# Bias sums over 64 rows in one product of ones, and the third tile's adapter transposed with the opening routing

## The chip, the cores and the metric

The kernel runs on one core of one Trainium2 chip. The metric is the device time of one execution in microseconds (us), here the median of three runs. The core has a matrix engine (TensorE, PE in the rows; its weight loads are PEld), a vector engine (VectorE, DVE), a scalar engine (ScalarE, ACT), GpSimd (POOL), and a queue engine (SyncE, SP) that issues most transfers. Each engine works through its own list in order; semaphores tie the lists together.

## The reference

Eight blocks (tiles) of 128 tokens, each token 512 wide. A first linear layer with a per-block low-rank adapter (rank 16), then a second layer whose output gets a contribution of two out of 16 experts per token, then the residual:

```python
lora_h = x @ A[slot]                                   # A, B chosen per block
y = x @ W.T + b + (lora_h @ B[slot]) * 2.0
base = y @ base_w.T + base_b
hidden = y @ A_ffn.T                                   # 64 wide
probs = softmax(y @ router_w.T)                        # 16 wide
topw, topi = top_k(probs, 2); topw = topw / (topw.sum() + 1e-6)
delta = sum_e combine[e] * (hidden @ B_ffn[e].T)
out = x + base + delta * 0.5
```

The first layer's bias `b` passes through the second layer, so each output column, and each column of `hidden` and of the router's logits, gets a constant: `sum_i b[i] * W2[i, n] + base_b[n]`, over 512 values of i.

## The kernel before, in words

**Folding.** W and the second layer's W2 (64 hidden, 16 router and 512 base columns: 592) are multiplied first, so that x meets one folded matrix P, 128 rows x 4 blocks k. All products run in a reduced-precision float format: each operand is split in a high part (a rounding copy, mostly on ScalarE) and a low part (value minus high, on VectorE or GpSimd), and each product is done as three: high x high, high x low, low x high. A pass over 592 columns is two matrix instructions of 296 columns, one for each half of a pair of PSUM banks (`halves`).

**Adapters.** C = B x W2 is made for all eight slots at once (`ps_c`, then `c_hi` and `c_lo`), and each tile's 16 rows are stacked by transfers into `c_stack`.

**Bias.** `bias_part_of(k)` on VectorE (L644) adds, for k = 0 to 3, the rows of W2 times the bias of their block into `bias_part` (128 rows x 592). What is left is a sum over 128 rows. It is split in `bp_hi` (ScalarE, L472) and `bp_lo` (VectorE, L679), and `bias()` on TensorE multiplies each with a matrix of ones, four matrix instructions of 296 columns. They stand in the last quarter of `x_other(0)`. ScalarE copies two rows of the sum (L549), VectorE makes the two constant rows of them (L693), which go into the first tile's adapter product and by a transfer (L315) into that of every other tile.

**Per tile t.** `x_first(t)` and `x_other(t)` are 12 matrix instructions each of 304 columns (4 blocks k, 3 products): the two halves of x P, the first with the adapter's 16 columns beside it. ScalarE and VectorE take these 16 columns out (`lora_hi`, L495; `lora_lo`, L701) in high and low parts beside each other in `routed`; TensorE turns them (`lora_transpose`, L960); ScalarE copies the result twice (`lora_t`, L502 and L503), and `lora_product(t)` (L970, L972) adds the adapter. VectorE takes out hidden and logits, makes the residual sum (`read_z`) and routes (`route`: maximum, two best, weights; exponentials in ScalarE's `exps`, L517). `routing_transpose(t)` (L990) turns hidden and weights of tile t. From t = 1 on it also turns the adapter part of tile t + 2, which then lies in the same tensor, so one transpose serves both; tiles 1 and 2 have a `lora_transpose` of their own. `routing_rows(t)` on ScalarE (L530, L531) copies the turned rows out; the weights go through memory (`spread_routing` on SP: out at L325, back in two copied forms at L338), VectorE multiplies them with hidden (`weigh`, L760) and the expert products of 512 columns follow in `iteration(t)`.

**What sets the order.** Everything is written out by hand, engine by engine: the order of the calls is the order of execution. The calls on TensorE around the change, in the main part:

```
x_first(0) x_other(0) lora_first_transpose x_first(1) lora_first_product x_other(1) lora_transpose(1)
x_first(2) routing_transpose(0) lora_product(1) x_other(2) lora_transpose(2) x_first(3) lora_product(2)
x_other(3) routing_transpose(1) x_first(4) ...
```

**GpSimd's list.** low part of x for tile 2, then a wait for `bp_lo` (`bpl_done`), low part of x for tile 3 (L380), adapter columns 2 (L390, L392), low part of the first expert quarter (L398), adapter 3, two more quarters, then for t = 4 to 7 adapter columns and low part of x. `x_first(4)` on TensorE waits for the low part of x of tile 4. VectorE makes one expert quarter itself (L657, behind `route(1)`).

Of the kernel before, what the change touches and what calls it, by code (L numbers as in the profile page):

```python
# [11 lines left out]
F32 = mybir.dt.float32  # L12
F32R = mybir.dt.float32r
# [5 lines left out]
P = 128  # L19
# [43 lines left out]
def adaln_ffn_kernel(nc, x_t, x_n, w_cat, tables, slots, b1, b2, experts, out):  # L63
    with ExitStack() as ctx:
        def sb(name, shape, dt=F32):
            return ctx.enter_context(nc.sbuf_tensor(name, shape, dt))
# [4 lines left out]
        def sem(name):  # L71
            return ctx.enter_context(nc.semaphore(name))
# [24 lines left out]
        c_hi = sb("c_hi", [P, W2N], F32R)  # L97
        c_lo = sb("c_lo", [P, W2N], F32R)
        bias_part = sb("bias_part", [P, W2N])
        bp_hi = sb("bp_hi", [P, W2N], F32R)  # L100
        bp_lo = sb("bp_lo", [P, W2N], F32R)
        bias_hi = sb("bias_hi", [FT, W2N], F32R)
        low_row = sb("low_row", [FT, 1])
        c_stack = sb("c_stack", [FT, NT, W2N], F32R)
# [104 lines left out]
        ch_done = sem("ch_done")  # L209
        cl_done = sem("cl_done")  # L210
        bias_step = sem("bias_step")
        bph_done = sem("bph_done")
        bpl_done = sem("bpl_done")
        pe_bias = sem("pe_bias")
# [204 lines left out]
        def _(act):  # L419
# [26 lines left out]
            def split_experts(q):  # L446
                js = slice(q * GC // 4, (q + 1) * GC // 4)
                act.wait_ge(in_exp[q], 16)
                nc.scalar.activation(e_hi[:, js, :], exp_raw[:, js, :], ACT.Copy).then_inc(eh_done, 1)
# [16 lines left out]
            x_hi_part(2)  # L466
            x_hi_part(3)
            split_experts(0)
            act.wait_ge(pe_c, 1)
            nc.scalar.activation(c_hi[:, :], w2_cols(ps_c), ACT.Copy).then_inc(ch_done, 1)  # L470
            act.wait_ge(bias_step, KC)
            nc.scalar.activation(bp_hi[:, :], bias_part[:, :], ACT.Copy).then_inc(bph_done, 1)  # L472
            def lora_first():
                z = z_lora[0]
                act.wait_ge(pe_first, 1)
# [10 lines left out]
            def lora_hi(t):  # L486
                z = z_lora[t % 2]
                act.wait_ge(pe_first, t + 1)

                if t in (3, 4):  # L490
                    act.wait_ge(pe_ht, t - 1)
                elif t >= 5:
                    act.wait_ge(pe_rt, t - 3)
                h_parts = routed[:, t % 2, T_H:P].rearrange("p (r b) -> p b r", b=2)
                nc.scalar.activation(h_parts[:, 0, :].bitcast(F32R), ps_z[t % 2][:, z:z + R], ACT.Copy,  # L495
                                     scale=LORA_SCALE).then_inc(hh_done, 1)
# [8 lines left out]
            def lora_t_alone(t):  # L505
                act.wait_ge(pe_ht, t + 1)
                lora_t(t, ps_ht)
# [49 lines left out]
            lora_hi(2)  # L557
            routing_rows(0)
            exps(1)
            lora_t_alone(2)  # L560
            act.wait_ge(in_xt[2], 16)
            x_hi_part(4)
            lora_hi(3)
# [27 lines left out]
        def _(dve):  # L591
# [46 lines left out]
            def bias_part_of(k):  # L638
                if k == 0:
                    dve.wait_ge(in_b, 32)  # L640
                    dve.wait_ge(first_set, 1)
                else:
                    dve.wait_ge(bias_step, k)
                nc.vector.scalar_tensor_tensor(out=bias_part[:, :], in0=w_raw[:, k, D:], scalar=b1_col[:, k:k + 1],  # L644
                                               in1=(b2_rows if k == 0 else bias_part)[:, :],
                                               op0=ALU.mult, op1=ALU.add).then_inc(bias_step, 1)

            def folded_lo(n):
                dve.wait_ge(ph_done, n + 1)
                m = FOLDS[n]  # L650
                nc.vector.tensor_tensor(p_lo[:, m, R:MVN], w2_cols(pairs[m]),
                                        p_hi[:, m, R:MVN].bitcast(F32), ALU.subtract).then_inc(pl_done, 1)

            def split_experts_lo(q):
# [6 lines left out]
            x_lo_early(1)  # L661
            bias_part_of(0)
            bias_part_of(1)
            folded_lo(0)
            folded_lo(1)
            dve.wait_ge(lbh_done, 1)
# [3 lines left out]
                                    ALU.subtract).then_inc(lbl_done, 1)  # L670
            folded_lo(2)
            folded_lo(3)
            bias_part_of(2)
            bias_part_of(3)
            dve.wait_ge(ch_done, 1)
            nc.vector.tensor_tensor(c_lo[:, :], w2_cols(ps_c), c_hi[:, :].bitcast(F32),
                                    ALU.subtract).then_inc(cl_done, 1)
            dve.wait_ge(bph_done, 1)
            nc.vector.tensor_tensor(bp_lo[:, :], bias_part[:, :], bp_hi[:, :].bitcast(F32),  # L679
                                    ALU.subtract).then_inc(bpl_done, 1)  # L680

            def lora_first_lo():
# [140 lines left out]
        def _(pe):  # L823
# [85 lines left out]
            def x_other(t):  # L909
                out_cols, cols = other_half[t % 2]  # L910

                x_side(t, out_cols, cols, bias_within=t == 0).then_inc(pe_x, 1)

            def x_side(t, out_cols, cols, bias_within=False):
                par = t % 2
                x_h, x_l = x_his[t % XB], x_los[t % XB]
                for k in range(KC):
                    if k == KC - 1 and bias_within:
                        bias()
                    if t == 0 and k == 0:  # L920
                        pe.wait_ge(pl_done, KC)
                    for n, (lhs, rhs) in enumerate(((x_h, p_hi), (x_h, p_lo), (x_l, p_hi))):
                        last = mm(ps_z[par][:, out_cols], lhs[:, k, :], rhs[:, k, cols],
                                  k == 0 and n == 0, k == KC - 1 and n == 2)
                return last

            def bias():
                pe.wait_ge(consts, 4)
                pe.wait_ge(bph_done, 1)
                pe.wait_ge(bpl_done, 1)  # L930
                halves(ps_b, BANK - W2H, W2H, ones[:, :], bp_hi[:, :], True, False)
                halves(ps_b, BANK - W2H, W2H, ones[:, :], bp_lo[:, :], False, True).then_inc(pe_bias, 1)

            def lora_first_transpose():
                pe.wait_ge(hh_done, 1)
# [16 lines left out]
            def lora_transpose(t):  # L952
                pe.wait_ge(hh_done, t + 1)
                pe.wait_ge(hl_done, t + 1)
                pe.wait_ge(ht_done, t)

                if t >= 2:
                    pe.wait_ge(ht_again_done, t - 1)
                    pe.wait_ge(rt_done, t - 1)
                nc.tensor.transpose(ps_ht, routed[:, t % 2, T_H:P], ident[:, :]).then_inc(pe_ht, 1)  # L960

            def lora_product(t):
# [13 lines left out]
            def routing_transpose(t):  # L976
                cols = SMALL
                pe.wait_ge(weights_done, t + 1)
                if 3 <= t + 2 < NT:
                    cols = P  # L980
                    pe.wait_ge(ht_set, 2)
                    pe.wait_ge(hh_done, t + 3)
                    pe.wait_ge(hl_done, t + 3)

                if t >= 1:
                    pe.wait_ge(rt_done, t)
                if t < 2:
                    pe.wait_ge(ht_done, t + 2)
                    pe.wait_ge(ht_again_done, t + 1)
                nc.tensor.transpose(ps_rt[0:cols, :], routed[:, t % 2, 0:cols], ident[:, :]).then_inc(pe_rt, 1)  # L990
# [44 lines left out]
            x_other(1)  # L1035
            lora_transpose(1)
            x_first(2)
            routing_transpose(0)
            lora_product(1)
            x_other(2)  # L1040
            lora_transpose(2)
            x_first(3)
            lora_product(2)
            x_other(3)
# [52 lines left out]
```

## Time and profile before

| | |
|---|---|
| three runs | 102.5, 101.35, 102.38 us; median 102.38 us |
| profiled execution | 101.29 us |
| its span, first to last instruction | 99.5 us |
| TensorE busy | 95.7 us, 96% of the span, 572 matrix instructions |
| VectorE, ScalarE, GpSimd busy | 66.0, 41.5, 21.4 us |
| chain that ended last | TensorE 93%, transfers 3% |

The profile is of one execution. The span leaves out 1.79 us of the execution's own time (101.29 - 99.5). Times in the rows below count from the span's start, in us. A matrix instruction's duration contains its way through the array; in an unbroken stream the distance from start to start is what it costs. A wait on TensorE holds the weight load that comes first.

### The profile page before, as it was taken

How to read it: one execution, taken by the hardware profiler on the slowest of the kernel's cores; microseconds unless marked ns; L12 is line 12 of the kernel's file. 1: busy time of each engine (PE TensorE's matmuls, PEld its weight loads, DVE VectorE, ACT ScalarE, POOL GpSimd, SP SyncE). 2: the span in 40 equal slices, each digit the busy share in tenths (PEclk: the TensorE clock that was granted, in tenths of full speed). 3: DMA queues.
4: the chain of work that ended last, by engine and by line, in shares of the span. 5: the costliest groups of instructions: out<-in, count | busy, mean ns of one | idle time of the engine just before them, and what ended most of it. 6: DMA issues, size and time to landing. Idle time of an engine off the chain costs nothing.

```text
span 99.5 us, 1812 instructions
## 1 busy us (share of the span) xinstructions
PE 95.7 (96%) x572; PEld 87.1 (87%) x572; DVE 66.0 (66%) x184; ACT 41.5 (42%) x101; POOL 21.4 (21%) x34
## 2 busy tenths in 40 slices
PE   6899999999999999999999999999999999999990
PEld 6799999999999999998898799887788787888980
DVE  5669996997475885995997577257949274572101
ACT  1713536878787545754442510551434031040000
POOL 4100004325999965107022000000000000000000
PEclk9999999999999999999999999999999999999999
DMA  2999669999357777892593472616237082020311
GB/s 47 337 362 389 188 132 338 303 403 362 78 93 195 209 227 158 235 209 56 142 243 114 128 204 102 213 37 194 107 95 234 25 232 84 0 105 0 112 53 53
DMA packets 8443, 16.92 MB, mean 170 GB/s; under 512 B 1571, under 2 KB 4131, under 8 KB 8434
## 3 DMA queue, kind: packets, MB, share of 16 engines
q1 hardware_dynamic: 7762, 16.41, 55.2%
q10 hardware_dynamic: 640, 0.40, 1.3%
q8 instruction: 5, 0.08, 0.4%
q14 instruction: 4, 0.03, 0.1%
q0 software_dynamic: 32, 0.00, 0.0%
HBM read 13.28 MB, written 2.16 MB: 155 GB/s over the span
## 4 chain that ended last, share of the span: by engine, by line
PE 93%; DMA 3%; DVE 0%; ACT 0%; issue 0%
PE pair L825 90%; DMA w_raw_all<-w_cat 3%; PE pair L970 1%; PE pair L972 1%; PE pair L990 1%; DVE xn L819 0%; ACT w_hi_all L425 0%; PE pair L960 0%; PE pair L949 0%; PE pair L947 0%; PE pair L939 0%
## 5 line engine op out<-in xcount | busy, mean ns | idle before, releaser
L825 PE MATMUL pair<-e_hi,w_hi_all 128*128 128x512 f32 (+1 forms) x72 | 27.1, 376 | 0.0
L825 PE MATMUL pair<-e_hi,w_lo_all 128*128 128x512 f32 (+1 forms) x72 | 26.7, 370 | 0.0
L825 PE MATMUL pair<-e_lo,w_hi_all 128*128 128x512 f32 (+1 forms) x72 | 26.7, 370 | 0.0
L538 ACT ACTIVATE w_hi_all<-exp_raw_all 128x512 fp32r<-128x512 f32 x16 | 9.7, 629 | 15.9 <-DVE exp_raw_all L760 15.8
L825 PEld LDWEIGHTS pair<-e_hi,w_lo_all 128*128 128x128 f32 x72 | 13.6, 188 | 2.5
L825 PEld LDWEIGHTS pair<-e_hi,w_hi_all 128*128 128x128 f32 x72 | 13.6, 188 | 2.5
L825 PEld LDWEIGHTS pair<-e_lo,w_hi_all 128*128 128x128 f32 x72 | 13.6, 189 | 2.0
L767 DVE TENSOR_TENSOR w_lo_all<-exp_raw_all,w_hi_all 128x512 fp32r<-128x512 f32 x16 | 10.4, 689 | 4.5 <-ACT w_hi_all L538 4.0
L760 DVE TENSOR_TENSOR exp_raw_all<-w_raw_all 128x512 f32<-128x512 f32 x16 | 11.0, 725 | 0.9 <-DMA w_raw_all<-spill 0.9
L774 DVE TENSOR_TENSOR xn<-pair,xn 128x512 f32<-128x512 f32 x7 | 4.8, 691 | 8.6 <-PE pair L825 8.6
L825 PE MATMUL pair<-p_hi,x_hi 128*128 128x304 f32 x32 | 10.0, 311 | 0.0
L825 PE MATMUL pair<-p_hi,w_hi_all 128*128 128x304 f32 x32 | 9.8, 308 | 0.0
L825 PE MATMUL pair<-p_lo,x_hi 128*128 128x304 f32 x32 | 9.7, 303 | 0.0
L825 PE MATMUL pair<-p_lo,w_hi_all 128*128 128x304 f32 x32 | 9.7, 302 | 0.0
L825 PE MATMUL pair<-p_hi,w_lo_all 128*128 128x304 f32 x32 | 9.7, 302 | 0.0
L825 PE MATMUL pair<-p_hi,x_lo 128*128 128x304 f32 x32 | 9.7, 302 | 0.0
L380 POOL TENSOR_TENSOR w_lo_all<-xt_raw,w_hi_all 128x512 fp32r<-128x512 f32 x4 | 5.2, 1297 | 14.5 <-ACT w_hi_all L443 11.4
L398 POOL TENSOR_TENSOR e_lo<-exp_raw_all,e_hi 128x1024 fp32r<-128x1024 f32 x3 | 7.2, 2400 | 0.0
L825 PE MATMUL pair<-w_hi_all 128*128 128x296 f32 x32 | 6.1, 301 | 0.4 <-ACT w_hi_all L425 0.4
L825 PEld LDWEIGHTS pair<-p_hi,w_hi_all 128*128 128x128 f32 x32 | 6.0, 188 | 0.3
L825 PEld LDWEIGHTS pair<-p_lo,w_hi_all 128*128 128x128 f32 x32 | 6.0, 189 | 0.2
L825 PE MATMUL pair<-w_lo_all,w_hi_all 128*128 128x296 f32 x32 | 6.1, 303 | 0.0
(107 smaller groups left out, 161.5 us busy)
## 6 DMA issues: line engine op xcount, KB each, us to landing
w_raw_all<-spill SPq DMA_DIRECT2D x16, 256.0 KB, 4.0
xt_raw<-x_t SPq DMA_DIRECT2D x4, 512.0 KB, 7.0
exp_raw_all<-experts SPq DMA_DIRECT2D x4, 512.0 KB, 8.4
xn<-x_n SPq DMA_DIRECT2D x4, 512.0 KB, 5.4
out<-xn SPq DMA_DIRECT2D x7, 256.0 KB, 2.8
w_raw_all<-w_cat SPq DMA_DIRECT2D x2, 552.0 KB, 6.5
c_stack<-c_hi SPq DMA_DIRECT2D x7, 74.0 KB, 3.8
c_stack<-c_lo SPq DMA_DIRECT2D x7, 74.0 KB, 4.2
```

The costliest lines, as they stand in the source:

```text
L380: pool.tensor_tensor(x_los[t % XB], xt_raw[:, t, :].rearrange("p (k n) -> p k n", k=KC), x_his[t % XB].bitcast(F32), ALU.subtract).then_in ...
L398: pool.tensor_tensor(e_lo[:, js, :], exp_raw[:, js, :], e_hi[:, js, :].bitcast(F32), ALU.subtract).then_inc(el_pool_done, 1)
L538: nc.scalar.activation(gt_hi[:, t % 2, js, :], g[:, js, :], ACT.Copy).then_inc(gh_done, 1)
L760: nc.vector.tensor_tensor(g[:, js, :], weight_rows[:, b, js, :], hidden[:, b, :].unsqueeze(1).to_broadcast([P, GH, P]), ALU.mult).then_inc ...
L767: nc.vector.tensor_tensor(gt_lo[:, t % 2, js, :], g[:, js, :], gt_hi[:, t % 2, js, :].bitcast(F32), ALU.subtract).then_inc(gl_done, 1)
L774: nc.vector.tensor_tensor(xn[:, t, :], ps_d[t % 2], xn[:, t, :], ALU.add).then_inc(out_done, 1)
L825: return nc.tensor.matmul(out_ap, lhs, rhs, start=first, stop=last)
L970: nc.tensor.matmul(ps_z[par][:, z_small[par]:BANK], ht[:, par, :], c_stack[0:HT, t, 0:border], start=False, stop=True, skip_group_check=True)
L972: nc.tensor.matmul(ps_z[par][:, BANK:BANK + W2N - border], ht[:, par, :], c_stack[0:HT, t, border:], start=False, stop=True, skip_group_ch ...
L990: nc.tensor.transpose(ps_rt[0:cols, :], routed[:, t % 2, 0:cols], ident[:, :]).then_inc(pe_rt, 1)
```

## The change

1. The bias sum is halved before it goes to TensorE. ScalarE copies the lower 64 rows of `bias_part` up to `bias_up`, VectorE adds the upper 64 rows, ScalarE takes the high part into rows 0 to 63 of `bp_split`, VectorE the low part into its rows 64 to 127. One product with ones then sums all 128 rows: two matrix instructions in place of four.
2. VectorE does `bias_part_of(2)` ahead of the folded low parts, no longer behind them. ScalarE's copy up stands ahead of `c_hi`.
3. `lora_transpose(2)` is gone. `routing_transpose(0)` now turns the adapter part of tile 2 too, in all 128 columns, and stands inside `x_other(2)` behind its first k; ScalarE's `lora_t(2)` reads it.

```diff
-        bp_hi = sb("bp_hi", [P, W2N], F32R)
-        bp_lo = sb("bp_lo", [P, W2N], F32R)
+        bias_up = sb("bias_up", [P // 2, W2N])
+        bp_split = sb("bp_split", [P, W2N], F32R)
...
@@ scalar
             split_experts(0)
+            act.wait_ge(bias_step, KC)
+            nc.scalar.activation(bias_up[:, :], bias_part[P // 2:, :], ACT.Copy).then_inc(bias_moved, 1)
             act.wait_ge(pe_c, 1)
             nc.scalar.activation(c_hi[:, :], w2_cols(ps_c), ACT.Copy).then_inc(ch_done, 1)
-            act.wait_ge(bias_step, KC)
-            nc.scalar.activation(bp_hi[:, :], bias_part[:, :], ACT.Copy).then_inc(bph_done, 1)
+            act.wait_ge(bias_added, 1)
+            nc.scalar.activation(bp_split[0:P // 2, :], bias_up[:, :], ACT.Copy).then_inc(bph_done, 1)
...
-                if t in (3, 4):
-                    act.wait_ge(pe_ht, t - 1)
-                elif t >= 5:
+                if t == 3:
+                    act.wait_ge(pe_ht, 2)
+                elif t >= 4:
                     act.wait_ge(pe_rt, t - 3)
...
             exps(1)
-            lora_t_alone(2)
+            lora_t(2, ps_rt[T_H:P, :])
...
@@ vector
             bias_part_of(1)
+            bias_part_of(2)
             folded_lo(0)
...
             folded_lo(3)
-            bias_part_of(2)
             bias_part_of(3)
+            dve.wait_ge(bias_moved, 1)
+            nc.vector.tensor_tensor(bias_up[:, :], bias_part[0:P // 2, :], bias_up[:, :],
+                                    ALU.add).then_inc(bias_added, 1)
             dve.wait_ge(ch_done, 1)
...
-            nc.vector.tensor_tensor(bp_lo[:, :], bias_part[:, :], bp_hi[:, :].bitcast(F32),
+            nc.vector.tensor_tensor(bp_split[P // 2:, :], bias_up[:, :], bp_split[0:P // 2, :].bitcast(F32),
                                     ALU.subtract).then_inc(bpl_done, 1)
...
@@ tensor
-                x_side(t, out_cols, cols, bias_within=t == 0).then_inc(pe_x, 1)
+                x_side(t, out_cols, cols, within=t in (0, 2)).then_inc(pe_x, 1)
...
+                    if k == 1 and t == 2 and within:
+                        routing_transpose(0)
...
-                halves(ps_b, BANK - W2H, W2H, ones[:, :], bp_hi[:, :], True, False)
-                halves(ps_b, BANK - W2H, W2H, ones[:, :], bp_lo[:, :], False, True).then_inc(pe_bias, 1)
+                halves(ps_b, BANK - W2H, W2H, ones[:, :], bp_split[:, :], True, True).then_inc(pe_bias, 1)
...
-                if 3 <= t + 2 < NT:
+                if t + 2 < NT:
                     cols = P
...
             x_first(2)
-            routing_transpose(0)
             lora_product(1)
             x_other(2)
-            lora_transpose(2)
             x_first(3)
```

VectorE between the early low parts of x and the first adapter part, before (L644 is a bias step, L651 a folded low part, L667 the adapters' low part, L676 `c_lo`, L679 `bp_lo`, L685 the first adapter part):

```order
L644 SCALAR_TENSOR_TENSOR bias_part<-w_raw_all,b_col,b_rows 128x592
L644 SCALAR_TENSOR_TENSOR bias_part<-w_raw_all,b_col,bias_part 128x592
L651 TENSOR_TENSOR p_lo<-pair,p_hi 128x592 x2
L667 TENSOR_TENSOR lb_lo<-lora_raw,lb_hi 128x8x4x16
L651 TENSOR_TENSOR p_lo<-pair,p_hi 128x592 x2
L644 SCALAR_TENSOR_TENSOR bias_part<-w_raw_all,b_col,bias_part 128x592 x2
L676 TENSOR_TENSOR c_lo<-pair,c_hi 128x592
L679 TENSOR_TENSOR bp_lo<-bias_part,bp_hi 128x592
L685 SCALAR_TENSOR_TENSOR h_first<-pair,h_first 128x16
```

and the same stretch of the changed kernel (whose lines have other numbers: L651 is the bias step, L658 the folded low part):

```order
L651 SCALAR_TENSOR_TENSOR bias_part<-w_raw_all,b_col,b_rows 128x592
L651 SCALAR_TENSOR_TENSOR bias_part<-w_raw_all,b_col,bias_part 128x592 x2
L658 TENSOR_TENSOR p_lo<-pair,p_hi 128x592 x2
L675 TENSOR_TENSOR lb_lo<-lora_raw,lb_hi 128x8x4x16
L658 TENSOR_TENSOR p_lo<-pair,p_hi 128x592 x2
L651 SCALAR_TENSOR_TENSOR bias_part<-w_raw_all,b_col,bias_part 128x592
L683 TENSOR_TENSOR bias_up<-bias_part,bias_up 64x592
L686 TENSOR_TENSOR c_lo<-pair,c_hi 128x592
L689 TENSOR_TENSOR bp_split<-bias_up,bp_split 64x592
L695 SCALAR_TENSOR_TENSOR h_first<-pair,h_first 128x16
```

One bias step has moved ahead of the folded low parts, and the addition stands between the last bias step and `c_lo`.

TensorE from the end of `x_first(2)` into `x_other(2)`, before (L990 is the routing transpose, L970 and L972 the adapter product of tile 1):

```order
L825 MATMUL pair<-p_hi,w_lo_all 128x304
L990 MATMUL pair<-ident,routed 80x128 [waits ht_again_done,ht_done,weights_done]
L970 MATMUL pair<-c_stack,ht 128x304 [waits stacked1,ht_set,stacked_bias,ht_again_done,ht_done]
L972 MATMUL pair<-c_stack,ht 128x288
L825 MATMUL pair<-p_hi,w_hi_all 128x304
L825 MATMUL pair<-p_lo,w_hi_all 128x304
```

and changed (L998 is the routing transpose):

```order
L835 MATMUL pair<-p_hi,w_lo_all 128x304
L978 MATMUL pair<-c_stack,ht 128x304 [waits stacked1,ht_set,stacked_bias,ht_again_done,ht_done]
L980 MATMUL pair<-c_stack,ht 128x288
L835 MATMUL pair<-p_hi,w_hi_all 128x304
L835 MATMUL pair<-p_lo,w_hi_all 128x304
L835 MATMUL pair<-p_hi,w_lo_all 128x304
L998 MATMUL pair<-ident,routed 128x128 [waits hl_done,ht_done,hh_done,ht_again_done,ht_set,weights_done]
```

The transpose has moved five instructions later and now waits for the adapter parts of tile 2 as well (`hh_done`, `hl_done`).

## Rows read from the trace of the kernel before

**Rows 1.** The page: granted TensorE clock in 40 slices of the span.

```profile
PEclk9999999999999999999999999999999999999999
```

**Rows 2.** Waits of TensorE: engine line waited for: us, times, longest.

```profile
PE pair L825 <- PEq L1090: 0.8, 1, 0.8
PE pair L825 <- ACT w_hi_all L425: 0.4, 1, 0.4
```

**Rows 3.** The chain that ended last, in order: start us, us, what.

```profile
32.62 0.11 PE pair L960
```

**Rows 4.** Timeline of TensorE: start us, us, engine line op out<-in xcount.

```profile
23.90 0.43 PE L825 MATMUL pair<-bp_hi,ones 128*128 128x296 f32 x2
...
24.44 0.30 PE L825 MATMUL pair<-p_hi,x_hi 128*128 128x304 f32 x1
...
30.39 0.27 PE L990 MATMUL pair<-ident,routed 128*80 128x128 f32 x1
```

**Rows 5.** Timeline of the weight loads: bias, `x_first(1)`, second k of `x_other(2)`, `x_first(4)`.

```profile
23.77 0.33 PEld L825 LDWEIGHTS pair<-bp_hi,ones 128*128 128x128 f32 x2
...
24.86 0.19 PEld L825 LDWEIGHTS pair<-p_hi,x_hi 128*128 128x128 f32 x1
...
31.06 0.19 PEld L825 LDWEIGHTS pair<-p_hi,w_hi_all 128*128 128x128 f32 x1
...
36.20 0.19 PEld L825 LDWEIGHTS pair<-p_hi,x_hi 128*128 128x128 f32 x1
```

**Rows 6.** Timeline of VectorE around the bias; in brackets idle before, and its releaser.

```profile
14.37 0.83 DVE L644 SCALAR_TENSOR_TENSOR bias_part<-w_raw_all,b_col,bias_part 128x592 f32<-128x592 f32 x1
16.12 1.60 DVE L651 TENSOR_TENSOR p_lo<-pair,p_hi 128x592 fp32r<-128x592 f32 x2 [0.91 <-ACT p_hi L453]
...
19.59 1.49 DVE L644 SCALAR_TENSOR_TENSOR bias_part<-w_raw_all,b_col,bias_part 128x592 f32<-128x592 f32 x1
...
22.72 0.78 DVE L679 TENSOR_TENSOR bp_lo<-bias_part,bp_hi 128x592 fp32r<-128x592 f32 x1
...
23.71 0.77 DVE L779 TENSOR_TENSOR c_stack<-pair,c_stack 16x592 fp32r<-16x592 f32 x1
```

**Rows 7.** Timeline of ScalarE in the same stretch.

```profile
19.68 1.06 ACT L449 ACTIVATE e_hi<-exp_raw_all 128x1024 fp32r<-128x1024 f32 x1
...
21.98 0.70 ACT L472 ACTIVATE bp_hi<-bias_part 128x592 fp32r<-128x592 f32 x1 [0.16 <-DVE bias_part L644]
```

**Rows 8.** Timeline of GpSimd, 19 to 36 us.

```profile
19.14 1.31 POOL L380 TENSOR_TENSOR w_lo_all<-xt_raw,w_hi_all 128x512 fp32r<-128x512 f32 x1 [1.77 <-ACT w_hi_all L443]
23.57 1.29 POOL L380 TENSOR_TENSOR w_lo_all<-xt_raw,w_hi_all 128x512 fp32r<-128x512 f32 x1 [3.12 <-DVE bp_lo L679]
...
25.12 0.32 POOL L392 TENSOR_TENSOR p_lo<-lora_raw,p_hi 128x64 fp32r<-128x64 f32 x1
...
33.36 1.22 POOL L392 TENSOR_TENSOR p_lo<-lora_raw,p_hi 128x64 fp32r<-128x64 f32 x1
34.55 1.28 POOL L380 TENSOR_TENSOR x_lo<-xt_raw,x_hi 128x512 fp32r<-128x512 f32 x1
```

**Rows 9.** Timeline of VectorE, 30 to 42 us.

```profile
30.80 0.18 DVE L701 SCALAR_TENSOR_TENSOR routed<-pair,routed 128x16 fp32r<-128x16 f32 x1 [1.34 <-ACT routed L495]
...
33.18 1.22 DVE L657 TENSOR_TENSOR e_lo<-exp_raw_all,e_hi 128x1024 fp32r<-128x1024 f32 x1
...
40.72 1.28 DVE L760 TENSOR_TENSOR exp_raw_all<-w_raw_all 128x512 f32<-128x512 f32 x2
```

**Rows 10.** Timeline of ScalarE, 30 to 32 us.

```profile
30.80 0.27 ACT L530 ACTIVATE w_raw_all<-pair 16x128 f32<-16x128 f32 x1
...
31.50 0.31 ACT L517 ACTIVATE probs<-routed,neg_max 128x16 f32<-128x16 f32 x1
```

**Rows 11.** Timeline of SP's queue, 31 to 36 us.

```profile
34.06 1.14 SPq L338 DMA_DIRECT2D w_raw_all<-spill x2
```

**Rows 12.** The transfers of L338, 16 of them, to landing.

```profile
DMA to landing us min/median/max: 3.4/4.0/5.5
```

More of the change, by code:

```diff
@@ L211, in adaln_ffn_kernel @@
         bias_step = sem("bias_step")
+        bias_moved = sem("bias_moved")
+        bias_added = sem("bias_added")
         bph_done = sem("bph_done")
@@ L910, in x_other, with x_side @@
                 out_cols, cols = other_half[t % 2]
-                x_side(t, out_cols, cols, bias_within=t == 0).then_inc(pe_x, 1)
-            def x_side(t, out_cols, cols, bias_within=False):
+                x_side(t, out_cols, cols, within=t in (0, 2)).then_inc(pe_x, 1)
+            def x_side(t, out_cols, cols, within=False):
                 par = t % 2
@@ L917, in x_side @@
                 for k in range(KC):
-                    if k == KC - 1 and bias_within:
+                    if k == KC - 1 and t == 0 and within:
                         bias()
+                    if k == 1 and t == 2 and within:
+                        routing_transpose(0)
                     if t == 0 and k == 0:
@@ L955, in lora_transpose @@
                 pe.wait_ge(ht_done, t)
-                if t >= 2:
-                    pe.wait_ge(ht_again_done, t - 1)
-                    pe.wait_ge(rt_done, t - 1)
                 nc.tensor.transpose(ps_ht, routed[:, t % 2, T_H:P], ident[:, :]).then_inc(pe_ht, 1)
```

## The prediction

> **What bounds the kernel now.** I read the page first: the granted TensorE clock stands at its full level, 2.4 GHz, in all 40 slices [rows 1], so no term below comes from the clock. The waits of TensorE come next: it waited twice in the whole execution, 0.8 us for the start and 0.4 us for the first split [rows 2]. From then on it runs without a gap to the last product. So TensorE's list of instructions is the time. A matrix instruction taken out gives back its distance from start to start; a wait put in front of one is paid in full; every other engine costs nothing until it makes TensorE wait. The rest of my reading is therefore the timeline, engine by engine, at the places that the change touches: how early is each thing that TensorE takes, and how much later does it come now.
>
> **What goes.** The four bias products start at 23.90 and the next product at 24.44 [rows 4]: 0.54 us for four, 0.135 each. Two go: -0.27. The lone transpose of tile 2 has 0.11 us on the chain [rows 3]: -0.11. The transpose that takes over its work has 128 columns of weights where it had 80, but streams the same 128 (30.39 in rows 4), so I add nothing for it; the bounds are nothing and the 0.11 of a whole transpose. Together -0.38, the gain if no wait appears.
>
> **The bias chain.** Before, it was: last bias step, high part on ScalarE, low part on VectorE. Now it is: last step, copy up, addition, high, low, all in a row, over four hand-overs between two engines.
> - The step that moves forward goes in front of the folded low parts at 16.12, where VectorE was idle for 0.91 us; a step takes 0.83 [rows 6]. It costs nothing; the cover is that gap, and a few hundredths more would only delay low parts.
> - The last step now starts where the last but one did, at 19.59. That instruction took 1.49 us there, 0.66 more than its like at 14.37 [rows 6], while GpSimd ran its own subtraction from 19.14 to 20.45 [rows 8]. The bounds are 0.83 and 1.49. I take 1.49, since the same operation on the same kind of tile meets the same GpSimd instruction at the same moment. It ends at 21.08. ScalarE is free since 20.74 [rows 7].
> - Half the rows don't make it cheaper: over 16 rows VectorE's subtraction took 0.77, over 128 rows 0.78 [rows 6]. A ScalarE pass over 592 columns took 0.70 [rows 7]. A hand-over is 0.04 (high part ends 21.98 + 0.70 = 22.68, low part starts 22.72). So: copy up 21.12 to 21.82, addition 21.86 to 22.64, high part 22.68 to 23.38, low part 23.42 to 24.20. Before, the low part ended at 23.50. The chain ends 0.70 later.
> - `c_hi` and `c_lo` fill the holes between (ScalarE from 21.8, VectorE from 22.6), and what stands behind them, the transfers of `c_stack`, are wanted only by `lora_product(1)`.
> - TensorE loads the bias weights at 23.77 [rows 5], now not before 24.24: a wait of 0.47. If the last step took 0.83, the load could go at 23.58 and there would be no wait. Bounds 0 and 0.47; I take 0.47. After the two products that went, TensorE is at +0.20.
>
> **What hangs on the chain.** `x_first(1)` loads at 24.86 [rows 5] and waits for the first tile's low adapter rows, 23.71 + 0.77 = 24.48 [rows 6], a slack of 0.38. Their place is behind `bp_lo`. If they shift by the whole 0.70 they are there at 25.18 + 0.04, and TensorE wants them at 24.86 + 0.20 = 25.06: 0.16 more. But before they stood 0.2 us off the end of `bp_lo`'s slot, so less than 0.70 reaches them. I take 0 and keep 0.16 for the range.
>
> **The routing transpose.** It now stands behind the first k of `x_other(2)`, whose second k loads at 31.06 [rows 5]. A transpose ahead of that is gone (-0.11) and TensorE is at +0.20: 31.15. It needs the low adapter part of tile 2, 30.80 + 0.18 = 30.98 [rows 9], which follows `x_first(2)` and so shifts by 0.20 as well: 31.18, with the hand-over 31.22. A wait of 0.07; bounds 0 and 0.15.
>
> **GpSimd's list.** It waits for `bp_lo` before its next subtraction, at 23.57 [rows 8], and is then packed up to the low part of x for tile 4, 34.55 to 35.83. Shifted by 0.70 that ends at 36.53. `x_first(4)` waits for it and loads at 36.20 [rows 5], now at 36.20 + 0.20 - 0.11 + 0.07 = 36.36. Whether that wait comes hangs on one instruction. GpSimd's short subtraction at 33.36 took 1.22 us where its like at 25.12 took 0.32 [rows 8]; VectorE's expert quarter ran from 33.18 to 34.40 [rows 9], started 0.18 earlier, and GpSimd's ended 0.18 behind it. Now both are later. GpSimd's comes at 34.06. VectorE's follows the routing of tile 1, which waits for ScalarE's exponentials, which now stand behind the copies of the later transpose: load 31.22, 0.13 to the product (23.77 to 23.90), 0.27 for it [rows 4], 0.04: 31.66 in place of 30.80; the exponentials 0.54 to 0.70 behind that, at 32.20 to 32.36 in place of 31.50 [rows 10]; so the expert quarter at 33.88 to 34.04. VectorE is still first, by 0.02 to 0.18. Then it holds GpSimd to 35.10 or later, the low part of x ends about 36.57, and TensorE waits 0.25. If GpSimd is first it saves its 0.90 and nobody waits. Bounds 0 and 0.37; I take 0.25.
>
> The Trainium skill, "SBUF — State Buffer", section "Who interferes with whom", has a rule for this: a VectorE instruction with two SBUF inputs and a GpSimd instruction that reads SBUF exclude each other, and the one that starts second is blocked for the whole of the first. By that rule, both long rows are blocked instructions (the trace agrees: 1.49 beside 0.83, 1.22 beside 0.32), and the sum below holds; if they were chance, the bias wait and the one at `x_first(4)` would both be absent and the sum would be -0.38 + 0.07.
>
> **The sum.** -0.27 - 0.11 + 0.47 + 0.07 + 0.25 = +0.41 us on the profiled execution's 101.29, so 101.7. With every wait at its lower bound it is -0.38, at its upper -0.38 + 0.63 + 0.15 + 0.37 = +0.77. Behind `x_first(4)` I cost nothing: GpSimd and ScalarE idle again before the low part of x for tile 5, and the 35 us of expert products have no wait to lengthen. The runs shown are 101.35, 102.38 and 102.5: the profiled execution lies with the fastest, 1.1 us under the median, and nothing in the profile says where a new median falls. I put the number between 101.7 and 102.38 + 0.41 = 102.8, at 102.2.
>
> **Rivals.**
> 1. Bias wait yes, `x_first(4)` no, because GpSimd gets in ahead of VectorE: +0.16. For it: the margin is a tenth of a us. On the two bases 101.45 to 102.55.
> 2. The waits stay away and the whole -0.38 is seen: 100.9 to 102.0. For it: the last bias step meets GpSimd only if GpSimd's subtraction isn't over; against it: nothing shifts that meeting, and the chain has two more passes and no slack left.
> 3. Slower by over 2%: the routing weights' way through memory. SP reads them back at 34.06 [rows 11], with 4.0 us median and 5.5 at most to landing [rows 12], and VectorE's first product with them stands at 40.72 without a gap [rows 9]. With the transpose's rows 0.86 later on ScalarE, the second of the two reads is issued about 35.5 and lands by 41.0 at the worst of the rows, against 41.1 wanted. From there each us late is up to a us of TensorE, which has nothing else to do before the expert products. To cost 2.05 us the landing must be at 43.2, 7.7 us after the issue; no row is that long.
> 4. That the change doesn't do what it says: the order shows two products and one transpose fewer, so I give it nothing of its own.
>
> **Chances and range.** Forecast 0.45, rival 1 0.33, rival 2 0.18, rival 3 0.02, the remaining 0.02 a gain over 2% that no term here makes. 2% (2.05 us) is about what a measurement of this kernel can tell from no change, and every case but the third is far inside it: same 0.96, faster 0.02, slower 0.02. The range runs from 101.0 (the profiled 101.29 less most of rival 2) to 103.1 (the slowest run, 102.5, with +0.6, the forecast with one more bound); the likeliest case's own is 101.6 to 102.9.
>
> **What would show it.** In the changed profile: the waits of TensorE list one for the low part of the bias at about 24.2, of some 0.45 us, and a small one at the moved transpose for VectorE's L711 or so; the bias step at 19.6 is 1.49 long; GpSimd's next subtraction starts at 24.2 to 24.3. A third wait of about 0.25 before the first product of `x_first(4)`, released by GpSimd, decides between the forecast and rival 1; there GpSimd's short subtraction near 34 is 1.2 or 0.3 long. The prediction is wrong if the addition and copy over 64 rows turn out shorter than over 128, if a step of the chain overlaps its neighbour, or if a wait appears in the expert stage.

## The result: half a microsecond slower

The changed kernel takes 102.54 us in the median of 22 runs, before 102.22 us in the median of 22: a ratio of 1.0049, 95% interval 1.0025 to 1.0073, or +0.5 us (the two medians alone differ by 0.32). Ratios, here and below, leave out executions more than 1.5% above their kernel's fastest. The change is within 2%, and clear of no change. The sum of the prediction was +0.41 on the profiled execution; the number that was written down, 102.2, lies under the median of 102.38 shown then, and so said "faster". The sign was lost after the sum, and three of its terms were off besides.

The profiled executions differ by 1.28 us (101.29 and 102.57), over twice the effect; their spans differ by 1.1 (99.5 and 100.6). Half of that is not the change: the first products of all, which nothing in it touches, went slower this time.

TensorE's first products, changed kernel (start us, us, what):

```profile
4.28 0.83 PE L835 MATMUL pair<-w_hi_all 128*128 128x296 f32 x2 [0.38 <-ACT w_hi_all L429]
4.90 0.69 PE L835 MATMUL pair<-w_lo_all,w_hi_all 128*128 128x296 f32 x2
5.40 0.69 PE L835 MATMUL pair<-w_hi_all,w_lo_all 128*128 128x296 f32 x2
```

and before:

```profile
4.25 0.51 PE L825 MATMUL pair<-w_hi_all 128*128 128x296 f32 x2 [0.35 <-ACT w_hi_all L425]
4.60 0.44 PE L825 MATMUL pair<-w_lo_all,w_hi_all 128*128 128x296 f32 x2
4.88 0.49 PE L825 MATMUL pair<-w_hi_all,w_lo_all 128*128 128x296 f32 x2
```

Two products that follow each other take 0.62 and 0.50 us from start to start (4.28 to 4.90 to 5.40) where before it was 0.35 and 0.28, and the same weight load, the first of `x_first(0)`, comes at 21.41 in place of 20.83. The views print a granted clock of 1.00, the upper level of 2.4 GHz, in this stretch of both traces, but there they have nothing to go by: the first clock entry in the trace, with 1.00, stands at 4.13 us before and at 6.06 us changed. In all eleven traces of this document that first entry lies between 4.12 and 6.64 us, and wherever the products behind 4.2 us run slow, they do so up to that entry: ahead of it one product of 296 columns takes 0.25 us from start to start, behind it 0.14. That is the pace of the lower level, 1.2 GHz, ahead of the entry (inferred from the pace; no entry gives the level there). What the engine did before is the same in both traces: thirteen products of constants from 0.78 to 3.89 us, then some 0.4 us of idling. So the start of an execution depends on when the clock rises, and the kernel before was profiled with almost the earliest rise of the eleven. The clock row of [rows 1] doesn't show this.

From here on I measure every trace from that load to the start of the last product: 96.56 - 20.83 = 75.73 us before, 97.70 - 21.41 = 76.29 changed, +0.56. That ruler leaves the start out, and its +0.56 lies within the interval of the ratio (+0.26 to +0.75 us).

**Where the 0.56 is.** The changed kernel's chain that ended last runs, between 20.26 and 24.88, no longer through TensorE but through the bias:

```profile
20.26 1.42 DVE bias_part L651
21.67 0.02 issue
21.69 0.71 ACT bias_up L474
22.40 0.02 issue
22.43 0.78 DVE bias_up L683
23.20 0.02 issue
23.23 0.71 ACT bp_split L478
23.94 0.02 issue
23.96 0.78 DVE bp_split L689
24.74 0.14 issue
24.88 0.93 PE pair L835 x5
```

The weight loads of the changed kernel, where TensorE's waits show (in brackets the idle time before):

```profile
24.85 0.30 PEld L835 LDWEIGHTS pair<-bp_split,ones 128*128 128x128 f32 x2 [0.46 <-issue]
...
25.85 0.19 PEld L835 LDWEIGHTS pair<-p_hi,x_hi 128*128 128x128 f32 x1 [0.22 <-issue]
...
31.38 0.19 PEld L980 LDWEIGHTS pair<-c_stack,ht 66*128 66x128 f32 x1
...
32.29 0.14 PEld L998 LDWEIGHTS pair<-ident,routed 128*128 128x128 f32 x1 [0.31 <-issue]
32.33 0.22 PEld L835 LDWEIGHTS pair<-p_hi,w_hi_all 128*128 128x128 f32 x1
...
37.34 0.19 PEld L835 LDWEIGHTS pair<-p_hi,x_hi 128*128 128x128 f32 x1
```

Against the load of `x_first(0)`, and against [rows 5], the bias weights come at 3.44 and not 2.94 (+0.50), `x_first(1)` at 4.44 and not 4.03 (+0.41, so 0.18 of it new, after the 0.27 of two products), the moved transpose 0.36 later than the row of loads in front of it would let it (31.38 and four steps of just under 0.14 give 31.93), and `x_first(4)` at 15.93 and not 15.37 (+0.56). So: -0.27 + 0.50 + 0.18 - 0.11 + 0.36 = +0.66, of which 0.1 comes back because the transpose runs beside the restart of the stream: the next load follows its own by 0.04 (32.29 to 32.33), where 0.14 is usual. That leaves the +0.56. `x_first(4)` did not wait: VectorE and GpSimd met otherwise than forecast.

VectorE and GpSimd, changed kernel, answering to [rows 6, 8, 9]:

```profile
20.17 1.49 DVE L651 SCALAR_TENSOR_TENSOR bias_part<-w_raw_all,b_col,bias_part 128x592 f32<-128x592 f32 x1
...
31.79 0.17 DVE L711 SCALAR_TENSOR_TENSOR routed<-pair,routed 128x16 fp32r<-128x16 f32 x1 [1.35 <-ACT routed L501]
...
34.80 1.22 DVE L664 TENSOR_TENSOR e_lo<-exp_raw_all,e_hi 128x1024 fp32r<-128x1024 f32 x1
```

```profile
19.72 1.31 POOL L384 TENSOR_TENSOR w_lo_all<-xt_raw,w_hi_all 128x512 fp32r<-128x512 f32 x1 [1.76 <-ACT w_hi_all L447]
...
34.60 0.32 POOL L396 TENSOR_TENSOR p_lo<-lora_raw,p_hi 128x64 fp32r<-128x64 f32 x1
34.88 2.29 POOL L384 TENSOR_TENSOR x_lo<-xt_raw,x_hi 128x512 fp32r<-128x512 f32 x1
```

GpSimd's short subtraction got in first (34.60, 0.32 long), but the next one, the low part of x itself, started 0.08 after VectorE's expert quarter and took 2.29 instead of 1.28. It ended at 37.17, 0.17 ahead of the load at 37.34. The rival "GpSimd gets in first and nobody waits" came true with the wrong reason: GpSimd saved 0.9 on the short subtraction and paid 1.0 one instruction later. And it got in first because VectorE was later than forecast: 34.80 is 34.22 on the time axis of before (0.58 of later start taken off), where 33.88 to 34.04 was worked out. The transposed rows, and with them the routing on VectorE, followed a transpose that waited 0.29 us longer than forecast.

### The profile page after: what moved, and what is told of

Read it like the earlier page. It is cut to its first block, busy times and chain, and to the rows that moved or that the text cites. A ratio compares the mean times of both kernels' runs of the same rounds, so it can differ in the third digit from the quotient of the medians.

```text
span 100.6 us, 1808 instructions
## 1 busy us (share of the span) xinstructions
PE 96.5 (96%) x569; PEld 87.4 (87%) x569; DVE 66.9 (67%) x185; ACT 41.9 (42%) x102; POOL 21.8 (22%) x34
## 4 chain that ended last, share of the span: by engine, by line
PE 85%; DVE 6%; DMA 3%; ACT 2%; issue 1%
PE pair L835 82%; DMA w_raw_all<-w_cat 3%; DVE p_lo L658 2%; DVE bias_part L651 1%; PE pair L998 1%; PE pair L978 1%; PE pair L980 1%; DVE bp_split L689 1%; DVE bias_up L683 1%; ACT bp_split L478 1%; ACT bias_up L474 1%; ACT p_hi L457 1%; DVE lb_lo L675 1%; DVE xn L829 0%; ACT w_hi_all L429 0%
## 5 line engine op out<-in xcount | busy, mean ns | idle before, releaser
L835 PE MATMUL pair<-w_hi_all,w_lo_all 128*128 128x296 f32 x32 | 6.3, 308 | 0.0
```

The source lines that it names most:

```text
L835: return nc.tensor.matmul(out_ap, lhs, rhs, start=first, stop=last)
```

## Experiments

Each was timed in five rounds beside the kernel before. "Ruler" is the stretch from the first load of `x_first(0)` to the last product, 75.73 us before, 76.29 changed.

**1. The bias part alone.** The transposes are put back:

```diff
-                    if k == 1 and t == 2 and within:
-                        routing_transpose(0)
...
             x_first(2)
+            routing_transpose(0)
             lora_product(1)
             x_other(2)
+            lora_transpose(2)
```

> Only the bias part of the change; the transposes stand as before. Theory A (the waits of the changed trace are the cost, each paid in full by TensorE): -0.27 for two products, +0.50 at the bias weights, +0.18 at x_first(1), nothing at the transposes: +0.4 us against before, ratio 1.004. Whether x_first(4) waits for GpSimd is open: it is 0 in the changed trace by 0.1 us. Rival B (the bias part is hidden and the moved transpose alone costs the time): -0.27, ratio 0.997, and no wait at the bias weights. Rival C (the difference is the first microseconds of an execution, which differ by 0.6 us between the two traces, not the change): ratio 1.000.

Measured: ratio 1.0099 (1.0055 to 1.0144), ruler 76.19, +0.46. Waits of 0.44 and 0.21 at the two loads, and at `x_first(4)` a small one:

```profile
36.54 0.14 PEld L999 LDWEIGHTS pair<-ident,routed 128*128 128x128 f32 x1
36.76 0.19 PEld L835 LDWEIGHTS pair<-p_hi,x_hi 128*128 128x128 f32 x1
```

The second load follows the first by 0.22, where 0.14 is usual: 0.08 of wait, for a low part of x that ends at 36.71 (the row 35.42, 1.29, below). Here it was GpSimd's first instruction, a copy, that VectorE's quarter held:

```profile
33.78 1.28 POOL L394 CAST p_hi<-lora_raw 128x64 fp32r<-128x64 f32 x1
35.13 0.32 POOL L396 TENSOR_TENSOR p_lo<-lora_raw,p_hi 128x64 fp32r<-128x64 f32 x1
35.42 1.29 POOL L384 TENSOR_TENSOR x_lo<-xt_raw,x_hi 128x512 fp32r<-128x512 f32 x1
```

Rival B (the bias part is hidden) falls, and so does rival C (only the start differs), since the ruler leaves the start out. The trace stands with theory A, but the runs are 0.5 us slower than the trace says.

**2. The transposes alone.** The bias is as before, four products and no fold of the rows.

> Only the transposes of the change; the bias as before. Theory A: -0.11 for the transpose that goes, and at the moved one a wait of 0.3 to 0.35 before its weights (of which some 0.08 is given back, since the transpose then runs beside the restart): +0.1 to +0.15 us against before, ratio 1.001. Rival B: the moved transpose costs all of the 0.5: ratio 1.005. If the wait is only what is late in data (adapter low part ready 30.98, load wanted 30.95), it is under 0.1 and the sum is about -0.05, ratio 0.9995.

Measured: ratio 1.0031 (0.9998 to 1.0065), ruler 75.87, +0.14. The load of the moved transpose:

```profile
31.80 0.14 PEld L989 LDWEIGHTS pair<-ident,routed 128*128 128x128 f32 x1 [0.31 <-issue]
```

A wait of 0.31 with no bias in the way, where lateness of the data alone would be under 0.1. So on the ruler the merge costs 0.14 where it was to give 0.11, and the two parts, +0.46 and +0.14, come to 0.60 against the +0.56 of both together. Rival B (0.5 for the transpose) falls on the ruler; the interval of the time can't tell 1.001 from 1.005.

**3. The same waits, another order.**

```diff
                 if t < 2:
                     pe.wait_ge(ht_done, t + 2)
                     pe.wait_ge(ht_again_done, t + 1)
+                if t == 0:
+                    pe.wait_ge(hl_done, 3)
```

(and the call ahead of it left out for t = 0).

> The changed kernel with the same waits at the moved transpose, but the one on tile 2's low adapter part called last. In the changed trace the low part is ready at 31.96 and the weights are loaded at 32.29, with two more wait instructions between. Theory A (after the wait that comes true last, TensorE still works through the waits behind it, about 0.1 us each): the gap before the weights shrinks from 0.31 to 0.1 to 0.2, and the time by 0.1 to 0.2 us against the changed kernel. Rival (the semaphore itself comes late): the gap stays 0.3.

Measured: ratio 1.0046 (1.0011 to 1.0081), ruler 76.57. The loads:

```profile
31.09 0.19 PEld L980 LDWEIGHTS pair<-c_stack,ht 66*128 66x128 f32 x1
...
31.79 0.14 PEld L1001 LDWEIGHTS pair<-ident,routed 128*128 128x128 f32 x1
...
37.00 0.19 PEld L835 LDWEIGHTS pair<-p_hi,x_hi 128*128 128x128 f32 x1 [0.17 <-POOL x_lo L384]
```

From L980 to the transpose it is 0.70 us, in the changed kernel 0.91 (31.38 to 32.29), without a wait 0.55. So the wait is 0.15 and not 0.36: 0.21 us went by the order of the calls alone. In this trace the low part is ready at 31.68 and the load follows 0.11 later, where it was 0.33 in the changed kernel (31.96 to 32.29). The time doesn't show it, and the ruler went up by 0.28, for two other reasons. In this execution the last bias step was held for longer,

```profile
19.56 1.82 DVE L651 SCALAR_TENSOR_TENSOR bias_part<-w_raw_all,b_col,bias_part 128x592 f32<-128x592 f32 x1
```

since GpSimd's subtraction began 0.12 ahead of it and not 0.45 (it waits for a copy on ScalarE, which here waited 0.22 us for the transfer of x). The bias load waited 0.78, 0.32 more. And `x_first(4)` waited 0.17 for GpSimd, the wait that the prediction had put there: with the transpose earlier, VectorE's quarter comes just ahead of GpSimd's short subtraction, the meeting that was forecast.

```profile
34.30 1.21 DVE L664 TENSOR_TENSOR e_lo<-exp_raw_all,e_hi 128x1024 fp32r<-128x1024 f32 x1
```

```profile
34.33 1.36 POOL L396 TENSOR_TENSOR p_lo<-lora_raw,p_hi 128x64 fp32r<-128x64 f32 x1
```

Together +0.32 + 0.17 - 0.21 = +0.28, the whole difference. So most of what the order of the waits gives back at the transpose was lost again at `x_first(4)`.

**4. Without the two extra passes.**

```diff
-            act.wait_ge(bias_step, KC)
-            nc.scalar.activation(bias_up[:, :], bias_part[P // 2:, :], ACT.Copy).then_inc(bias_moved, 1)
...
-            nc.scalar.activation(bp_split[0:P // 2, :], bias_up[:, :], ACT.Copy).then_inc(bph_done, 1)
+            nc.scalar.activation(bp_split[0:P // 2, :], bias_part[0:P // 2, :], ACT.Copy).then_inc(bph_done, 1)
```

> The changed kernel without ScalarE's copy up and VectorE's addition; the rows 64 to 127 of the bias partial sums are left out of the result. Two bias products, as changed. Theory A (the two extra passes are what is late; 0.70 + 0.78 + two hand-overs on a slack of 0.27, less the bias step that no longer stands in the way): no wait at the bias weights and none at x_first(1); against before -0.27 - 0.11 + what the moved transpose waits (0.3): -0.1 us, ratio 0.999, 0.6 us under the changed kernel. Rival (the late thing is the last bias step, held by GpSimd's subtraction): the step is at 1.49 us still, the chain ends as before, since before it had the same step; so this rival needs a wait to remain, of 0.2 or more.

Measured: ratio 1.000 (0.9972 to 1.0027), ruler 75.61, -0.12, no wait at the bias load nor at `x_first(1)`. Theory A gave -0.1. With the passes the same kernel is 0.68 slower on the ruler: that is what the copy and the addition cost as long as GpSimd holds the last bias step, which is 1.48 long here too. So the rival (the held step alone) falls.

**5. GpSimd kept away from the bias step.**

```diff
             lora_a_parts(1)
-            x_lo_part(2)
             pool.wait_ge(bpl_done, 1)
+            x_lo_part(2)
             x_lo_part(3)
...
             split_experts_lo(1)
-            split_experts_lo(3)
             for t in range(4, NT):
                 lora_a_parts(t)
                 x_lo_part(t)
+                if t == 4:
+                    split_experts_lo(3)
```

> The changed kernel, with GpSimd's low part of x for tile 2 held until the low part of the bias is done (so that it can't meet the last bias step), and GpSimd's expert quarter 3 moved behind the low part of x for tile 4. Theory A (the two engines exclude each other): the last bias step is 0.83 long, not 1.49; the bias weights wait under 0.1 in place of 0.5, x_first(1) not at all in place of 0.2; the moved transpose still 0.36; x_first(4) between 0 and 0.4, since GpSimd's low part of x then runs beside VectorE's expert quarter. From the first product of x_first(0) to the end: 75.73 us before, 76.29 changed, here 75.7 to 76.1. Rival (1.49 is the length of a step that late in the program, for another reason): the step stays 1.49 and the waits stay.

Measured: ratio 0.9991 (0.9959 to 1.0024), ruler 76.05. VectorE's last bias step, and three weight loads (bias, `x_first(1)`, `x_first(5)`):

```profile
20.06 0.83 DVE L651 SCALAR_TENSOR_TENSOR bias_part<-w_raw_all,b_col,bias_part 128x592 f32<-128x592 f32 x1
```

```profile
24.23 0.33 PEld L835 LDWEIGHTS pair<-bp_split,ones 128*128 128x128 f32 x2
...
25.17 0.19 PEld L835 LDWEIGHTS pair<-p_hi,x_hi 128*128 128x128 f32 x1
...
40.73 0.19 PEld L835 LDWEIGHTS pair<-p_hi,x_hi 128*128 128x128 f32 x1 [0.34 <-POOL x_lo L384]
```

0.83 in place of 1.49, so the rival falls, and the bias load has no wait: all four passes fit if the step isn't held. `x_first(1)` still waits 0.11, where I had expected nothing: its load follows the one before by 0.24 (24.93 to 25.17), without a wait 0.13. So 0.50 and 0.07 came back, and 0.34 of that turned into a new wait at `x_first(5)`, behind the quarter that I had moved; I had looked for it at `x_first(4)`.

**6. The bias part alone, with GpSimd's list reordered** (the second half of the diff of experiment 5).

> The bias part of the change alone, as in the run before, with GpSimd's expert quarter 3 moved behind the low part of x for tile 4. That run was 1.0099 of before, 0.5 us more than its trace shows (+0.46). Theory A (x_first(4) waits for GpSimd in most executions, and the traced one was a lucky one): with the low part secured the ratio falls to about 1.004. Rival (the surplus is in the first microseconds, where the clock or the first transfers differ from execution to execution): the ratio is 1.004 to 1.010 all the same and runs over the fastest show a longer start, not a wait.

Measured: ratio 1.0023 (0.999 to 1.0057), ruler 76.10, no wait at `x_first(4)`. The ratio fell, as theory A has it, but the two intervals just touch, the trace gained 0.09 only, and both this kernel and the one before had runs over 1.5 us above their fastest. The experiment decides nothing: what makes the runs of experiment 1 slower than their trace stays open.

**7. The transposes alone, with two waits in place of six.**

```diff
-                    pe.wait_ge(ht_set, 2)
-                    pe.wait_ge(hh_done, t + 3)
+                    if t >= 1:
+                        pe.wait_ge(ht_set, 2)
+                        pe.wait_ge(hh_done, t + 3)
                     pe.wait_ge(hl_done, t + 3)
...
-                if t < 2:
+                if t == 1:
                     pe.wait_ge(ht_done, t + 2)
```

> The bias as before, the transposes changed, and the moved transpose waiting only for the routing weights and the low adapter part (the other four conditions follow from waits that stand before it). Theory A (each wait instruction behind the one that comes true last costs TensorE 0.1 us): the gap before its weights shrinks from 0.31 to about 0.1, and from the first product of x_first(0) to the end it takes 75.6 to 75.7 us, against 75.87 with all waits and 75.73 before. In the time 0.999 of before, which five rounds can hardly tell. Rival (the data are late): the gap stays 0.3.

Measured: ratio 1.0025 (0.9981 to 1.0069), ruler 75.66, -0.07. Loads:

```profile
30.39 0.19 PEld L971 LDWEIGHTS pair<-c_stack,ht 66*128 66x128 f32 x1
...
31.09 0.14 PEld L990 LDWEIGHTS pair<-ident,routed 128*128 128x128 f32 x1
```

0.70 from one to the other, a wait of 0.15: as with the low part called last. The low part is ready at 30.97, 0.12 ahead of the load, so the rival (late data) falls. The merged transpose is worth its 0.07 only with a short list of waits; the ratio, with 1 inside its interval, can't tell such a difference.

**8. The whole change, with experiments 5 and 7.**

> The whole change with GpSimd's list reordered as in the first of these four and the moved transpose with two waits. Theory A: bias wait under 0.1, none at x_first(1), about 0.1 at the transpose, 0 to 0.4 at x_first(4): from x_first(0) to the end 75.5 to 75.9 us, ratio to before 0.998 to 1.002. If TensorE's waits just move on to x_first(4) in full, 76.2 and 1.005.

Measured: ratio 0.9983 (0.9954 to 1.0012), ruler 75.85, with the 0.34 at `x_first(5)` again, 0.15 at the transpose and 0.12 at `x_first(1)`, where none was expected.

**9. The same, with the fourth expert quarter on VectorE,** in the gap behind the routing of tile 2:

```diff
             read_z(2)
             route(2)
+            split_experts_lo(3)
             lora_lo(4)
```

(GpSimd's call of it is gone, and TensorE waits for VectorE's count in its place.)

> The kernel of e9_all with expert quarter 3 moved from GpSimd to VectorE, behind the routing of tile 2, where VectorE was idle for 1.3 us. In e9 the one wait left over 0.15 was 0.34 at x_first(5), for the low part of x for tile 5, which stood behind that quarter on GpSimd. Theory A (each wait of TensorE is paid in full and nothing else counts): that wait goes, and from the first product of x_first(0) to the end it takes 75.5 us, against 75.85 in e9, 75.73 before and 76.29 changed; ratio to before about 0.998, which five rounds can show only just. Rival (the wait moves on, to low adapter part 4 behind the new VectorE pass, or to the expert stage): 75.8 or more.

Measured: 101.54 us against 101.89, ratio 0.9961 (0.9927 to 0.9994), ruler 75.57. This one is faster than the kernel before. The ruler, -0.16, shows less than half of the 0.4 us. The changed kernel wasn't timed beside it; on the ruler it is 0.72 behind. The rival (75.8 or more) falls. Its weight loads and the new pass:

```profile
24.40 0.33 PEld L834 LDWEIGHTS pair<-bp_split,ones 128*128 128x128 f32 x2
...
25.09 0.13 PEld L950 LDWEIGHTS pair<-ident,h_first 128*98 128x98 f32 x1
25.40 0.19 PEld L834 LDWEIGHTS pair<-p_hi,x_hi 128*128 128x128 f32 x1 [0.18 <-issue]
```

```profile
37.56 1.22 DVE L662 TENSOR_TENSOR e_lo<-exp_raw_all,e_hi 128x1024 fp32r<-128x1024 f32 x1
38.86 0.17 DVE L709 SCALAR_TENSOR_TENSOR routed<-pair,routed 128x16 fp32r<-128x16 f32 x1
```

The quarter fits between the routing and the next adapter part. What is left is 0.18 at `x_first(1)` and 0.15 at the transpose. The 0.18 is ScalarE's: the bias step is done at 21.05, but the copy up stands behind an expert quarter.

```profile
20.16 1.06 ACT L451 ACTIVATE e_hi<-exp_raw_all 128x1024 fp32r<-128x1024 f32 x1
21.25 0.70 ACT L472 ACTIVATE bias_up<-bias_part 64x592 f32<-64x592 f32 x1
```

Added up as above (what the list saves, each wait of TensorE in full, 0.1 back at the transpose), the waits give the ruler of each of the nine experiments to within 0.04 us. The ratios are further off it, from -0.4 us (experiment 5) to +0.5 (experiment 1), with intervals of 0.3 to 0.45 us to either side; the start, which the ruler leaves out, can be a part of that, and how large a part isn't shown.

## Why the prediction was wrong, and where it was right

- **The number.** The failed step is the last of "The sum". It had +0.41 on the profiled execution, and then put the time half way between two bases, 101.29 and 102.38, which took 0.55 off and turned the sign against the median shown. The sum added to that median gives 102.8, slower as measured (102.54) and 0.25 above it. The profiled execution had almost the earliest rise of the clock among the traces (the first products above), which is worth up to 0.9 us at the first load of `x_first(0)`; the runs as a whole were not that fast. A change worked out on one execution is added to the median of the runs. The measured 102.54 lies inside the range of 101.0 to 103.1, which is too wide to test a mechanism.
- **What goes** was right: 0.27 and 0.11, and a transpose of 128 columns of weights costs no more than one of 80 (in the stream its load and the next are 0.14 to 0.15 apart with either: 30.25 to 30.39 before, 37.19 to 37.34 changed).
- **The bias chain** was right in mechanism: 0.47 forecast, 0.50 measured. Half the rows cost the same (0.77 over 64 rows, 0.78 over 128), the last step was 1.49, and experiments 4 and 5 each remove the wait, one by taking the two passes out, one by keeping GpSimd away. Only the hand-over into TensorE was 0.11 to 0.12 (low part ends 24.73, load 24.85) where I took 0.04 from two other engines. The size held with some luck: 1.49 was taken as the upper bound of the last step, and in experiment 3 it was 1.82, with the bias load 0.82 later than before. The other end was read wrongly too: with a step of 0.83 the copy up could not have begun before ScalarE was free at 20.74, so the load would have stood at 23.90 and not 23.58, a wait of 0.13 and not none; experiment 5 had none, since ScalarE was free earlier against `x_first(0)`.
- **`x_first(1)`**: 0 was taken, 0.16 kept as a bound; it was 0.18. The step that failed is "less than 0.70 reaches them": the low adapter rows started 0.24 after the end of the bias's low part, before 0.21, and moved by 0.68 (23.71 to 24.97, less the 0.58 of the start). They were done at 24.97 + 0.77 = 25.74, and TensorE's hand-over of 0.11 again made the rest.
- **The moved transpose** is the term that was mis-sized most: 0.07 forecast, bound 0.15, measured 0.36. The low part was there at 31.96, 0.03 after its place in the list, as worked out. The other 0.33 lies between the data and the load, where I had 0.04: experiments 3 and 7 take 0.21 of it away by changing only which wait is called when, or how many there are. In the eight traces with the moved transpose the load follows the low part by 0.32 to 0.33 us where two waits are called behind it (the changed kernel, experiments 2, 4 and 5), and by 0.11 to 0.13 where it is the last (3, 7, 8 and 9).
- **`x_first(4)`**: 0.25 forecast, 0 in the changed trace, 0.17 and 0.08 in two others. The wait exists and hangs on which of three GpSimd instructions meets VectorE's quarter, a matter of 0.2 us. That none came in the changed kernel is luck, of the mis-sized transpose above all: it moved VectorE behind GpSimd's short subtraction. My alternative, that GpSimd going first saves everybody, had no basis: in every one of the eleven traces one of its instructions is lengthened beside VectorE's quarter, by 0.3 to 1.05 us.
- The misses partly cancel (0.03 + 0.18 + 0.29 too few, 0.25 too many, and 0.1 for the transpose beside the restart: +0.15 in all), so +0.41 against +0.56 on the ruler is closer than its parts.
- "The 35 us of expert products" is a misreading without effect: they run from 43.70 to the end, 53 us, and the list has no wait there in either trace.

The Trainium skill, "SBUF — State Buffer", "Who interferes with whom", says that the order of issue decides who blocks, and that the other blocks fully. The runs agree in five places: the bias step of 1.49 and 1.82 against 0.83, GpSimd's low part of 2.29 against 1.28, its copy of 1.28 against 0.23, its short subtraction of 1.22 against 0.32 [rows 8]; and experiment 5 takes the 1.49 away by keeping GpSimd out. The traces also show when the blocked instruction ends: the bias step 0.63 us after GpSimd's, with 1.49 (20.45 to 21.08, 21.03 to 21.66) as with 1.82 (20.75 to 21.38), 0.20 less than its own 0.83.

## What to carry to other kernels

Where one engine's list is the time, price a removed instruction by its distance from start to start, and then follow what feeds the next wait: here two products of 0.14 us were bought with two passes of 0.7 us on a chain that had 0.27 us of slack. Put the condition that comes true last at the end of an instruction's waits, and leave out those that an earlier wait already implies (the traces show 0.21 us for it at one place; the times are too coarse to show it). And before two engines are given work with two operands in SBUF at the same moment, look which of the two stands on the critical chain.

## What the runs showed of the hardware

- On TensorE, with the stream stopped, changing the order of six waits moved a load by 0.21 us, and so did cutting them to two. TensorE's load came 0.11 to 0.13 us after the end of the VectorE instruction it waited for, if that wait was the last in its list, and about 0.05 us after GpSimd's (36.71 to 36.76 in experiment 1, 40.69 to 40.73 in 5), against 0.03 to 0.04 between VectorE and ScalarE.
- A transpose that is issued as the stream restarts costs about 0.1 us less than in the stream: the next load follows after 0.04 us, not 0.14.
- A GpSimd copy of 64 columns took 1.28 us beside VectorE's subtraction of two SBUF operands, and 0.23 alone: it need not have two operands itself.
- The eleven traces begin with the same products and reach the first load of `x_first(0)` between 20.80 and 21.68 us. The first products run at half the pace until the first clock entry, at 4.12 to 6.64 us, although the views print a granted clock of 1.00 from the start.
